# New order of the instructions in phase one of a fused RWKV + mixture-of-experts kernel, and an earlier release of one PSUM tile

## Chip, cores, metric

One core of a Trainium2 chip. The metric is the device time of the whole kernel in microseconds. Before: median 914.38 us of 3 runs (911.5 to 915.5).

## The reference

Two layers, all fp32, on x of 4 x 1024 x 256: an RWKV attention layer with 16 heads of 16 channels, and a mixture of 8 experts with two chosen for each token. Each stands behind a layer norm and inside a residual.

```python
xin = x; x = norm(x)                              # over the 256 channels
xx = shift(x) - x                                # previous token minus this one
r, k, v = (x + xx * maa_r) @ Wr.T, (x + xx * maa_k) @ Wk.T, (x + xx * maa_v) @ Wv.T
g = gelu((x + xx * maa_g) @ Wg.T)
for each chunk of tokens:                        # scan, state is N x N for each head
    y = (r @ k * Wmat) @ v + r @ state * wb
    state = ws * state + (k * wk) @ v
yn = (y - mean(y)) / sqrt(var(y) + eps)          # for each head
x1 = xin + (yn * ln_w + ln_b) * g @ Wo.T
d = norm(x1); probs = softmax(d @ gate.T)        # two experts for each token, 320 places in each for a batch
out = x1 + sum over its experts: probs * (silu(d @ w1) * (d @ w3)) @ w2
```

## The kernel before, in words

Phase one (`phase_a`) works through 4096 tokens in 16 blocks of 256 tokens. For each block it normalizes x (statistics on VectorE `stats1`, rstd on GpSimd `norm1`, scaling on ScalarE `normed1`), transposes it on TensorE (`turn1`, L1187, into the PSUM tile pX), copies it out (`turned1`, L731), mixes it with the shifted x (`shifted`, `mixing` on VectorE, `mixed_g` on GpSimd) and projects r, k, v, g (`project_*`, L1147 and L1172). The attention in a block: `scores` (L1214, two halves a and b, four row tiles of 32 rows each) into pS, `mask` on VectorE (L917, four groups a half), `within` (L1248, four groups a half, column tiles), `across` (L1239, with the state, 32 x 32 tiles), `outer` (L1205, column tiles, the new state's products). y is copied and squared by ScalarE (`keep_y`, `square_y`); `group_sums` (L1261) sums the squares for each head into pX; `group_rstd` (L717, L718) makes 1/sqrt of them as an exponential of a logarithm; then `normed_y` (VectorE), `scaled` (ScalarE), `gated` (GpSimd), `project_o` (L1272), `residual` and `stats2` (VectorE), `norm2` (GpSimd), `normed2` (ScalarE), `turn2` (L1281), `logits` (L1289), `logit_max`, `logit_exp`, `best_two`, `tally`, `count` (L1299, L1300), `slots`, and `scatter`: four indirect DMAs on GpSimd (L564) that send the rows of a block to the expert's places in memory. `weight_high` and `weight_low` split the first expert's weights in two parts, beside all that.

Phase two runs the experts from those places. Its first chunk of 512 rows begins inside phase one's tail (`early_*`).

Each engine runs its own hand-written list of calls, in order: a loop over c, whose calls carry the block that they work on, and a written-out tail. The engines meet only at semaphores. So the order of the lists sets what is late. The loops begin at different values of c, and so how many statistics and normalizations stand ahead of the first block is set there too. The decay tables (`decay_logs` and `bonus` on VectorE, `decay_tables` on ScalarE) are made inside the first turns of the loops.

Two rules of the code matter for the change. pX is one PSUM tile, used in turn by turn1, group_sums and project_o. Before the change turn1 waits for the exponential, though only the logarithm reads pX:

```python
wait(pe, grstd_ready, b - 1)                                     # turn1, L1184
chain.link(nc.scalar.activation(grstd[:], pX[:], ACT.Ln, ...))   # group_rstd, L717
nc.scalar.activation(grstd[:], grstd[:], ACT.Exp, scale=-0.5)    # L718, then grstd_ready
```

And `within(b, 0, 0)` waits for the first mask, `scores_b` for the fourth:

```python
pe.wait_ge(attm_ready[g], TPS * b + t + 1)                       # within, L1246
pe.wait_ge(attm_ready[HGS - 1], TPS * b + 1)                     # scores_b, L1227
```

Of the kernel before, what the change touches and what calls it, by code (L numbers as in the profile page):

```python
# [24 lines left out]
ACT = mybir.ActivationFunctionType  # L25
# [6 lines left out]
N = C // H  # L32
# [228 lines left out]
def phase_a(nc, sb, ps, ctx, sem, ident, x, maa, decay_row, decay_ch, u_row, weights, lnw, lnb, gateT, disp, out,  # L261
# [120 lines left out]
    ysq_ready, ssum_done, yn_ready = sem("ysq_ready"), sem("ssum_done"), sem("yn_ready")  # L382
    y_ready, grstd_ready = sem("y_ready"), sem("grstd_ready")
    z_ready, zg_ready, wo_done = sem("z_ready"), sem("zg_ready"), sem("wo_done")
# [4 lines left out]
    count_done, slot_ready, sent = sem("count_done"), sem("slot_ready"), [sem(f"sent{k}") for k in range(2)]  # L389
    dve_chain, pool_chain, act_chain = sem("dve_chain"), sem("pool_chain"), sem("act_chain")  # L390
    taken_ready = sem("taken_ready")
# [78 lines left out]
    def on_gpsimd(pool):  # L470
# [108 lines left out]

        for c in range(-3, TAIL):  # L580
            scatter(c - 4)
            norm2(c - 2)
            norm1(c + 3)
            if c == -3:
                tables()
            gated(c - 1)
            decayed_r(c + 1)
            mixed_g(c + 1)
            if c == -1:
                empty_rows()  # L590
            weight_low(c - 6)
            chain.reset()

        scatter(11)
        chain.reset()
        norm2(13)
        gated(14)
        weight_low(10)
        scatter(12)
        chain.reset()  # L600
        norm2(14)
        gated(15)
        scatter(13)
        chain.reset()
        norm2(15)
        weight_low(11)
        scatter(14)
        chain.reset()
        early_index()
        scatter(15)  # L610
        chain.reset()
        weight_low(9)

    def on_scalar(act):
        chain = Chain(act, act_chain)
        for dst, src in ((lam_row, decay_row), (lam_ch, decay_ch)):
# [93 lines left out]

        def group_rstd(b):
# [80 lines left out]
        normed2(13)  # L792
        turned2(13)
        keep_y(15)
        square_y(15)
        early_hi(0)
        early_hi(1)
        group_rstd(15)
        logit_exp(13)
        normed2(14)  # L800
        scaled(15)
        early_gate(0)
        turned2(14)
        early_hidden_hi(0)
        early_gate(1)
        weight_high(11)
        early_hidden_hi(1)
        logit_exp(14)
        early_gate(2)
        normed2(15)  # L810
        turned2(15)
        early_hidden_hi(2)
        logit_exp(15)
        early_gate(3)
        early_gate(4)
        early_hidden_hi(3)
        early_hidden_hi(4)
        early_gate(5)
        early_gate(6)
        early_hidden_hi(5)  # L820
        early_hidden_hi(6)

    def on_vector(dve):
# [221 lines left out]

        for c in range(-4, TAIL):
            best_two(c - 3)
            mask(c, 0, 0)
            mask(c, 0, 1)
            mask(c, 0, 2)  # L1050
            mask(c, 0, 3)
            masked_kv(c)
            if c == -1:
                decay_logs()
                center_v()
                head_parity()
            shifted(c + 1)
            mixing(c + 1, 0)
            normed_y(c - 1)
            state_a(c)  # L1060
            tally(c - 3)
            mixing(c + 1, 1)
# [12 lines left out]
            slots(c - 3)  # L1075
            logit_max(c - 2)
            residual(c - 1)
            stats2(c - 1)
            state_b(c)
            chain.reset()  # L1080

        best_two(12)
        mask(15, 0, 0)
        mask(15, 0, 1)
        mask(15, 0, 2)
        mask(15, 0, 3)
        normed_y(14)
        tally(12)
        masked_kv(15)
        state_a(15)  # L1090
        mask(15, 1, 0)
# [4 lines left out]
        chain.reset()  # L1096
        residual(14)
        early_lo(0)
        early_lo(1)
        stats2(14)  # L1100
        logit_max(13)
        normed_y(15)
        best_two(13)
        tally(13)
        slots(13)
        chain.reset()
        early_hidden(0)
        residual(15)
        early_hidden_lo(0)
        early_hidden(1)  # L1110
        logit_max(14)
        stats2(15)
        best_two(14)
        tally(14)
        early_hidden(2)
        early_weight()
        slots(14)
        chain.reset()
        early_hidden_lo(1)
        logit_max(15)  # L1120
        state_b(15)
        best_two(15)
        tally(15)
        early_hidden(3)
        slots(15)
        chain.reset()
        early_hidden_lo(2)
        early_hidden(4)
        early_hidden_lo(3)
        early_hidden_lo(4)  # L1130
        early_hidden(5)
        early_hidden(6)
        early_hidden_lo(5)
        early_hidden_lo(6)
# [3 lines left out]
    def on_tensor(pe):  # L1138
# [192 lines left out]
        for c in range(-1, TAIL):  # L1331
            within(c - 1, 1, 2)
            count(c - 4)
            within(c - 1, 1, 3)
            turn2(c - 3)
            turn_k(c)
            project_o(c - 2)
            logits(c - 3)
            project_v(c)
            group_sums(c - 1)  # L1340
            scores_a(c)
            project_g(c)
# [12 lines left out]
            within(c, 1, 1)  # L1355

        within(14, 1, 2)
        count(11)
        within(14, 1, 3)
        turn2(12)  # L1360
        turn_k(15)
        project_o(13)
        logits(12)
        project_v(15)
        group_sums(14)
        scores_a(15)
        project_g(15)
        outer(15)
        across(15, 0)
        within(15, 0, 0)  # L1370
        scores_b(15)
# [9 lines left out]
        turn2(13)  # L1381
        project_o(14)
        early_turn(0)
        early_turn(1)
        logits(13)
# [12 lines left out]
        early_up(4)  # L1398
        count(15)
        early_up(5)  # L1400
        early_up(6)
# [535 lines left out]
```

## Time and profile before

| | |
|---|---|
| median of 3 runs | 914.38 us (911.5 to 915.5) |
| the profiled execution | 918.7 us, span 917.0 us |
| TensorE matmul busy | 848.2 us (93%) |
| TensorE weight load busy | 706.8 us (77%) |
| VectorE | 460.4 us (50%) |
| ScalarE | 490.7 us (54%) |
| GpSimd | 462.2 us (50%) |
| mean granted TensorE clock | 0.989 |

The span is the time between the first and the last instruction of the profiled execution. Busy time is the time in which an engine works; TensorE's ends are modelled. A row's start is in us from the span's start. In the timelines neighbouring instructions of one form are merged, and a bracket gives the idle time of the engine before the row, and what ended it. A step here is the time between the same instruction of two neighbouring blocks.

### The profile page before, as it was taken

What the parts mean: (1) busy time and instruction counts of PE and PEld (TensorE: products, weight loads), DVE (VectorE), ACT (ScalarE), POOL (GpSimd) and SP (SyncE); (2) the same over time, 40 slices, a digit from 0 to 9 for tenths busy, and PEclk for the clock granted to TensorE, in tenths of its full rate; (3) what the DMA queues carried; (4) which work ended last, traced back from release to release, by engine and by line L of the source; (5) the groups of instructions that cost most, each with busy time, mean ns of one, the idle gap of its engine ahead of it and who ended that gap; (6) DMA issues with size and microseconds to landing.
All of it is one profiled execution on the core that took longest, in us unless ns stands there. A gap on an engine that the chain in (4) does not pass through costs nothing. (4 is left out here: it accounts for less than half of the span.)

```text
span 917.0 us, 18900 instructions
## 1 busy us (share of the span) xinstructions
PE 848.2 (93%) x6791; PEld 706.8 (77%) x6792; DVE 460.4 (50%) x1174; ACT 490.7 (54%) x875; POOL 462.2 (50%) x497
## 2 busy tenths in 40 slices
PE   2899999999999999897999999999799999999995
PEld 1667777777677777787889789879689879889885
DVE  5767777777777766333442342442242443352330
ACT  2578777777788768253443453443353344353331
POOL 4534666677765756456237345237237136447024
PEclk9999999999999999899999999999999999999998
DMA  4572121112211122447025327025225214414013
GB/s 150 223 277 65 49 88 49 49 60 67 81 37 37 37 67 77 158 120 174 1 81 87 112 64 133 3 81 88 72 81 88 71 41 109 90 41 48 13 18 40
DMA packets 50464, 73.94 MB, mean 81 GB/s; under 512 B 5056, under 2 KB 42176, under 8 KB 50368
## 3 DMA queue, kind: packets, MB, share of 16 engines
q1 hardware_dynamic: 35488, 53.46, 17.6%
q0 software_dynamic: 14592, 19.18, 12.3%
q8 instruction: 62, 1.02, 0.4%
q14 instruction: 34, 0.28, 0.1%
q10 hardware_dynamic: 288, 0.01, 0.0%
HBM read 38.41 MB, written 34.22 MB: 79 GB/s over the span
## 5 line engine op out<-in xcount | busy, mean ns | idle before, releaser
L1547 POOL TENSOR_TENSOR wlo<-wraw,whi 128x448 fp32r<-128x448 f32 x84 | 102.6, 1225 | 209.9 <-ACT whi L1604 209.9
L1824 PE MATMUL p<-xh,whi 128*128 128x512 f32 (+1 forms) x504 | 190.9, 379 | 12.8 <-DVE xl L1723 4.9
L1826 PE MATMUL p<-xh,wlo 128*128 128x512 f32 (+1 forms) x504 | 190.4, 378 | 0.0
L1825 PE MATMUL p<-xl,whi 128*128 128x512 f32 (+1 forms) x504 | 189.6, 376 | 0.0
L1741 DVE TENSOR_TENSOR hid<-gated,p 128x512 f32<-128x512 f32 (+1 forms) x126 | 81.1, 643 | 211.6 <-ACT gated L1618 211.6
L1555 POOL DMA_INDIRECT out<-ysb,index x80 | 125.4, 1568 | 91.2 <-ACT ysb L1640 57.3
L1618 ACT ACTIVATE gated<-p 128x512 f32<-128x512 f32 (+1 forms) x126 | 71.0, 563 | 186.3 <-PE p L1826 186.3
L1844 PE MATMUL py<-whi,hh 128*128 128x256 f32 x469 | 135.2, 288 | 6.6 <-DVE hl L1043 3.5
L1846 PE MATMUL py<-whi,hl 128*128 128x256 f32 x469 | 132.6, 283 | 0.0
L1845 PE MATMUL py<-wlo,hh 128*128 128x256 f32 x469 | 132.5, 283 | 0.0
L1824 PEld LDWEIGHTS p<-xh,whi 128*128 128x128 f32 x504 | 95.1, 189 | 33.3 <-issue 11.3
L1825 PEld LDWEIGHTS p<-xl,whi 128*128 128x128 f32 x504 | 95.3, 189 | 18.9
L1826 PEld LDWEIGHTS p<-xh,wlo 128*128 128x128 f32 x504 | 94.9, 188 | 18.9
L1640 ACT ACTIVATE ysb<-py,weight 128x256 f32<-128x256 f32 x67 | 31.8, 475 | 121.7 <-PE py L1846 105.9
L917 DVE TENSOR_TENSOR attm<-pS,dmask 128x512 f32<-128x512 f32 x128 | 79.7, 683 | 32.0 <-remote 22.4
L1844 PEld LDWEIGHTS py<-whi,hh 128*128 128x128 f32 x469 | 89.1, 190 | 7.7 <-DVE hl L1043 3.9
L1749 DVE TENSOR_TENSOR hl<-hid,hh 128x512 fp32r<-128x512 f32 (+1 forms) x126 | 88.9, 706 | 3.7 <-ACT hh L1627 3.1
L1845 PEld LDWEIGHTS py<-wlo,hh 128*128 128x128 f32 x469 | 89.1, 190 | 0.4
L1846 PEld LDWEIGHTS py<-whi,hl 128*128 128x128 f32 x469 | 89.1, 190 | 0.0
L564 POOL DMA_INDIRECT disp<-row,slot_i x64 | 65.0, 1015 | 42.4 <-DVE slot_i L1025 26.3
L1723 DVE TENSOR_TENSOR xl<-pt,xh 128x512 fp32r<-128x512 f32 x33 | 22.7, 691 | 110.9 <-ACT xh L1610 103.2
L1627 ACT CAST hh<-hid 128x512 fp32r<-128x512 f32 (+1 forms) x126 | 72.8, 577 | 1.1 <-DVE hid L1741 1.1
(195 smaller groups left out, 1417.7 us busy)
## 6 DMA issues: line engine op xcount, KB each, us to landing
wraw<-in_w SPq DMA_DIRECT2D x24, 896.0 KB
disp<-wraw SPq DMA_DIRECT2D x16, 662.5 KB, 8.9
xtok<-disp SPq DMA_DIRECT2D x16, 530.0 KB, 5.1
x_ring<-in_x SPq DMA_DIRECT2D x16, 256.0 KB, 3.0
out<-x SPq DMA_DIRECT2D x16, 256.0 KB
xtok<-disp SPq DMA_DIRECT2D x8, 265.0 KB, 6.0
out<-ysb,index POOLq DMA_INDIRECT x80
disp<-row,slot_i POOLq DMA_INDIRECT x64
```

The costliest lines, as they stand in the source:

```text
L917: nc.vector.tensor_tensor(attm[g][:], pS[:, :, g // 2, g % 2, :], group_mask(g), ALU.mult).then_inc(attm_ready[g], 1)
L1547: nc.gpsimd.tensor_tensor(wlo[e.const % 2][m][:, cut], wraw[k][:, cut], whi[e.const % 2][m][:, cut].bitcast(F32), ALU.subtract).then_inc(w ...
L1555: nc.gpsimd.indirect_dma_start(out, bass.IndirectOffsetOnAxis(ap=index[e.const % 2][:, t:t + 1], axis=0), ysb[j % NY][:], None, compute_op ...
L1627: nc.scalar.copy(hh[(u * NCH + q) % 2][:, f, 0:w], hid[k][:, 0:w]).then_inc(hh_ready, 1)
L1741: nc.vector.tensor_tensor(hid[k][:, 0:w], gated[k][:, 0:w], p3[k][:, 0:w], ALU.mult).then_inc(hid_ready, 1)
L1749: nc.vector.tensor_tensor(hl[s][:, f, 0:w], hid[k][:, 0:w], hh[s][:, f, 0:w].bitcast(F32), ALU.subtract).then_inc(hl_ready, 1)
L1824: nc.tensor.matmul(dst[:, 0:w], hi[m][:, wcut], xh[xcut], start=(kt == 0), stop=False)
L1825: nc.tensor.matmul(dst[:, 0:w], hi[m][:, wcut], xl[xcut], start=False, stop=False)
L1826: ins = nc.tensor.matmul(dst[:, 0:w], lo[m][:, wcut], xh[xcut], start=False, stop=(kt == KT - 1))
L1844: nc.tensor.matmul(py[j % 2][:, 0:C], a, hi[:, cut], start=(f == 0), stop=False)
L1845: nc.tensor.matmul(py[j % 2][:, 0:C], a, lo[:, cut], start=False, stop=False)
L1846: ins = nc.tensor.matmul(py[j % 2][:, 0:C], b, hi[:, cut], start=False, stop=(f == FT - 1))
```

## The change

On TensorE the order of a step becomes: logits, turn_k, project_v, group_sums, scores_a, across, outer, within 0,0, turn1, project_g, scores_b, within 0,1 and 0,2, across, within 0,3, project_r, project_k, within 1,0 to 1,2, count, within 1,3, turn2, project_o. `group_rstd` is split, and turn1 waits for the logarithm's new semaphore. The lists of the other engines are reordered, their loops begin one turn later (GpSimd -2 instead of -3, VectorE -3 instead of -4), and with it the first blocks have one statistics less ahead. The work done is the same.

```diff
+        def group_log(b):
             if 0 <= b < STEPS:
                 act.wait_ge(ssum_done, b + 1)
...
                 wait(act, yn_ready, b)
-                chain.link(nc.scalar.activation(grstd[:], pX[:], ACT.Ln, scale=1.0 / N, bias=gn_eps[:, 0:1]))
+                nc.scalar.activation(grstd[:], pX[:], ACT.Ln, scale=1.0 / N, bias=gn_eps[:, 0:1]).then_inc(grlog_ready, 1)
+
+        def group_rstd(b):
+            if 0 <= b < STEPS:
+                act.wait_ge(grlog_ready, b + 1)
                 nc.scalar.activation(grstd[:], grstd[:], ACT.Exp, scale=-0.5).then_inc(grstd_ready, 1)
...
                 pe.wait_ge(xn_ready, b + 1)
-                wait(pe, grstd_ready, b - 1)
+                wait(pe, grlog_ready, b - 1)
```

TensorE's loop:

```diff
         for c in range(-1, TAIL):
-            within(c - 1, 1, 2)
-            count(c - 4)
-            within(c - 1, 1, 3)
-            turn2(c - 3)
+            logits(c - 3)
             turn_k(c)
-            project_o(c - 2)
-            logits(c - 3)
             project_v(c)
             group_sums(c - 1)
             scores_a(c)
+            across(c, 0)
+            outer(c)
+            within(c, 0, 0)
+            turn1(c + 1)
             project_g(c)
-            turn1(c + 1)
-            outer(c)
-            across(c, 0)
-            within(c, 0, 0)
             scores_b(c)
             within(c, 0, 1)
             within(c, 0, 2)
-            project_r(c + 1)
             across(c, 1)
             within(c, 0, 3)
+            project_r(c + 1)
             project_k(c + 1)
             within(c, 1, 0)
             within(c, 1, 1)
+            within(c, 1, 2)
+            count(c - 3)
+            within(c, 1, 3)
+            turn2(c - 2)
+            project_o(c - 1)
```

ScalarE's loop:

```diff
         for c in range(-2, TAIL):
+            logit_exp(c - 3)
+            weight_high(c - 4)
+            value(c)
+            group_log(c - 1)
+            group_rstd(c - 1)
             turned1(c + 1)
-            normed1(c + 2)
             column(c + 1)
             gate(c)
             scaled(c - 1)
             normed2(c - 2)
-            receptance(c + 1)
             if c == -1:
                 decay_tables()
             pairs(c + 1)
+            receptance(c + 1)
             key(c + 1)
+            normed1(c + 2)
+            turned2(c - 2)
+            square_y(c)
             keep_y(c)
-            square_y(c)
-            turned2(c - 2)
-            logit_exp(c - 2)
-            value(c + 1)
-            group_rstd(c)
-            weight_high(c - 4)
```

VectorE's and GpSimd's loops:

```diff
-        for c in range(-4, TAIL):
...
+        for c in range(-3, TAIL):
             mask(c, 1, 0)
             mask(c, 1, 1)
             mask(c, 1, 2)
             mask(c, 1, 3)
+            state_b(c)
             mixing(c + 1, 2)
-            stats1(c + 4)
+            slots(c - 3)
+            stats1(c + 3)
+            residual(c - 1)
+            logit_max(c - 2)
+            stats2(c - 1)
             if c == -1:
                 bonus(0)
             decayed_k(c + 1)
             if c == -1:
                 bonus(1)
                 slot_tables()
...
+            best_two(c - 2)
+            tally(c - 2)
+            mask(c + 1, 0, 0)
+            mask(c + 1, 0, 1)
+            mask(c + 1, 0, 2)
+            mask(c + 1, 0, 3)
+            masked_kv(c + 1)
+            state_a(c + 1)
+            if c == -2:
+                decay_logs()
+                center_v()
+                head_parity()
+            shifted(c + 2)
+            mixing(c + 2, 0)
+            normed_y(c)
+            mixing(c + 2, 1)
...
-        for c in range(-3, TAIL):
+        for c in range(-2, TAIL):
             scatter(c - 4)
             norm2(c - 2)
-            norm1(c + 3)
-            if c == -3:
+            norm1(c + 2)
+            if c == -2:
                 tables()
             gated(c - 1)
             decayed_r(c + 1)
+            weight_low(c - 6)
             mixed_g(c + 1)
             if c == -1:
                 empty_rows()
-            weight_low(c - 6)
```

The tails are reordered in the same way; on TensorE one more early product stands before turn2 of blocks 14 and 15.

```diff
         early_up(0)
         early_up(1)
         count(13)
+        early_up(2)
         turn2(14)
         project_o(15)
         logits(14)
-        early_up(2)
         early_up(3)
+        early_up(4)
         count(14)
         turn2(15)
         logits(15)
-        early_up(4)
+        early_up(5)
         count(15)
-        early_up(5)
         early_up(6)
```

## Rows read from the trace of the kernel before

**Rows 1.** Busy time by stretches: from:to, length, busy time of each engine, granted clock.

```profile
46.50:328.60 282.10, 268.41 (x3173) 203.09 (x3172) 212.79 (x676) 217.99 (x353) 179.71 (x235) 1.00 0.22 73
328.60:344.80 16.20, 14.09 (x205) 10.33 (x204) 10.34 (x33) 11.68 (x17) 8.74 (x13) 1.00 0.28 93
344.80:380.00 35.20, 29.94 (x130) 23.58 (x128) 22.44 (x90) 23.31 (x38) 21.25 (x29) 0.90 0.19 67
```

**Rows 2.** Waits, 0 to 400 us: who waited for whom, us, times, longest.

```profile
PE pX L1187 <- ACT grstd L718: 11.8, 14, 0.8
```

**Rows 3.** Timeline of TensorE, one step: start, length, what, [idle before].

```profile
205.39 1.03 PE L1261 MATMUL pX<-ysq,blockdiag 128*128 128x256 f32 x4
206.35 1.15 PE L1214 MATMUL pS<-r_pair,kT 32*128 32x256 f32 x16
207.43 1.99 PE L1147 MATMUL pB<-mixed,w_in_sb 128*128 128x256 f32 x8
210.26 0.63 PE L1187 MATMUL pX<-ident,xn 128*128 128x128 f32 x4 [0.84 <-ACT grstd L718]
210.82 0.46 PE L1205 MATMUL pA<-v_pad,k_dec 128*32 128x32 f32 x32
211.21 0.64 PE L1239 MATMUL pY<-r_dec,state 32*32 32x128 f32 x16
211.78 0.42 PE L1248 MATMUL pY<-attm,v_pad 128*32 128x128 f32 x8
212.53 1.15 PE L1214 MATMUL pS<-r_pair,kT 32*128 32x256 f32 x16 [0.33 <-DVE attm L917]
...
226.00 1.03 PE L1261 MATMUL pX<-ysq,blockdiag 128*128 128x256 f32 x4
```

**Rows 4.** Timeline of ScalarE in the same step.

```profile
205.59 0.59 ACT L699 COPY v_pad<-pA 128x512 f32<-128x512 f32 x1 [1.19 <-PE pA L1172]
...
207.49 0.69 ACT L717 ACTIVATE grstd<-pX,gn_eps 128x512 f32<-128x512 f32 x1
...
209.49 0.63 ACT L718 ACTIVATE grstd<-grstd 128x512 f32<-128x512 f32 x1
...
217.28 1.26 ACT L653 ACTIVATE r_pair<-pA,parity 128x512 f32<-128x512 f32 x2
```

**Rows 5.** Timeline of VectorE in the same step, the four masks of the first half.

```profile
210.00 2.48 DVE L917 TENSOR_TENSOR attm<-pS,dmask 128x512 f32<-128x512 f32 x4 [2.56 <-remote]
```

**Rows 6.** Timeline of TensorE and VectorE in block 1, before any scatter.

```profile
46.52 1.15 PE L1214 MATMUL pS<-r_pair,kT 32*128 32x256 f32 x16
...
47.74 2.48 DVE L917 TENSOR_TENSOR attm<-pS,dmask 128x512 f32<-128x512 f32 x4 [2.68 <-PE pS L1214]
```

**Rows 7.** Timeline of GpSimd: mixed g, then first and last of four indirect DMAs.

```profile
200.62 1.09 POOL L543 TENSOR_TENSOR mixed<-mixed,xT 128x512 f32<-128x512 f32 x1
...
204.13 1.11 POOL L564 DMA_INDIRECT disp<-row,slot_i  x1 [1.19 <-DVE slot_i L1025]
...
208.10 0.97 POOL L564 DMA_INDIRECT disp<-row,slot_i  x1 [0.30 <-issue]
```

**Rows 8.** Timeline of the start, 12 to 33 us.

```profile
12.06 0.75 DVE L875 BATCH_NORM_STATS2 st<-x_ring 128x6 f32<-128x256 f32 x2 [2.21 <-DMA x_ring<-in_x]
...
13.27 2.29 DVE L839 TENSOR_TENSOR dmask<-lam_row,lag 128x2048 f32<-128x2048 f32 x1
...
19.00 3.57 PE L1147 MATMUL pA<-mixed,w_in_sb 128*128 128x256 f32 x8 [9.69 <-DVE mixed L898]
...
22.61 0.59 ACT L644 COPY rT<-pA 128x512 f32<-128x512 f32 x1 [9.83 <-PE pA L1147]
...
25.68 0.19 ACT L628 ACTIVATE sdecay<-lam_ch 128x2 f32<-128x2 f32 x1
...
26.92 0.58 ACT L661 COPY kT<-pB 128x512 f32<-128x512 f32 x1
...
30.27 2.31 DVE L866 SCALAR_TENSOR_TENSOR dmask<-ident,u_sb,dmask 128x128 f32<-128x128 f32 x8
```

More of the change, by code:

```diff
@@ L382, in phase_a @@
     ysq_ready, ssum_done, yn_ready = sem("ysq_ready"), sem("ssum_done"), sem("yn_ready")
-    y_ready, grstd_ready = sem("y_ready"), sem("grstd_ready")
+    y_ready, grlog_ready, grstd_ready = sem("y_ready"), sem("grlog_ready"), sem("grstd_ready")
     z_ready, zg_ready, wo_done = sem("z_ready"), sem("zg_ready"), sem("wo_done")
@@ L389, in phase_a @@
     count_done, slot_ready, sent = sem("count_done"), sem("slot_ready"), [sem(f"sent{k}") for k in range(2)]
-    dve_chain, pool_chain, act_chain = sem("dve_chain"), sem("pool_chain"), sem("act_chain")
+    dve_chain, pool_chain = sem("dve_chain"), sem("pool_chain")
     taken_ready = sem("taken_ready")
@@ L596, in on_gpsimd @@
         norm2(13)
+        weight_low(10)
         gated(14)
-        weight_low(10)
         scatter(12)
@@ L601, in on_gpsimd @@
         norm2(14)
+        weight_low(9)
         gated(15)
@@ L605, in on_gpsimd @@
         norm2(15)
-        weight_low(11)
         scatter(14)
         chain.reset()
-        early_index()
         scatter(15)
         chain.reset()
-        weight_low(9)
+        early_index()
+        weight_low(11)
     def on_scalar(act):
-        chain = Chain(act, act_chain)
         for dst, src in ((lam_row, decay_row), (lam_ch, decay_ch)):
@@ L709, in normed1 @@
                 ins.then_inc(xn_ready, 1)
-        def group_rstd(b):
+        def group_log(b):
             if 0 <= b < STEPS:
@@ L780, in on_scalar @@
             pairs(c + 1)
+            receptance(c + 1)
             key(c + 1)
+            normed1(c + 2)
+            turned2(c - 2)
+            square_y(c)
             keep_y(c)
-            square_y(c)
-            turned2(c - 2)
-            logit_exp(c - 2)
-            value(c + 1)
-            group_rstd(c)
-            weight_high(c - 4)
+        logit_exp(12)
+        value(15)
+        group_log(14)
+        group_rstd(14)
+        normed2(13)
         scaled(14)
         gate(15)
-        normed2(13)
         turned2(13)
@@ L797, in on_scalar @@
         early_hi(1)
+        group_log(15)
+        logit_exp(13)
         group_rstd(15)
-        logit_exp(13)
+        early_gate(0)
         normed2(14)
         scaled(15)
-        early_gate(0)
+        weight_high(11)
+        early_gate(1)
         turned2(14)
+        early_gate(2)
         early_hidden_hi(0)
-        early_gate(1)
-        weight_high(11)
+        logit_exp(14)
         early_hidden_hi(1)
-        logit_exp(14)
-        early_gate(2)
+        early_gate(3)
         normed2(15)
@@ L813, in on_scalar @@
         logit_exp(15)
-        early_gate(3)
         early_gate(4)
         early_hidden_hi(3)
+        early_gate(5)
         early_hidden_hi(4)
-        early_gate(5)
+        early_hidden_hi(5)
         early_gate(6)
-        early_hidden_hi(5)
         early_hidden_hi(6)
@@ L1044, in early_hidden_lo @@
                                     ALU.subtract).then_inc(hl_ready, 1)
-        for c in range(-4, TAIL):
[L1047 to L1062, printed above, removed]
+        for c in range(-3, TAIL):
             mask(c, 1, 0)
@@ L1074, in on_vector @@
                 slot_tables()
[L1075 to L1079, printed above, removed]
-            chain.reset()
[L1082 to L1090, printed above, removed]
+            best_two(c - 2)
[14 more added lines that the diff above has]
+            mixing(c + 2, 1)
+            chain.reset()
         mask(15, 1, 0)
@@ L1097, in on_vector @@
         residual(14)
+        stats2(14)
         early_lo(0)
         early_lo(1)
-        stats2(14)
         logit_max(13)
-        normed_y(15)
         best_two(13)
         tally(13)
+        early_hidden(0)
+        normed_y(15)
         slots(13)
         chain.reset()
-        early_hidden(0)
+        early_hidden(1)
         residual(15)
+        stats2(15)
+        logit_max(14)
         early_hidden_lo(0)
-        early_hidden(1)
-        logit_max(14)
-        stats2(15)
+        early_hidden(2)
         best_two(14)
         tally(14)
-        early_hidden(2)
-        early_weight()
+        early_hidden_lo(1)
         slots(14)
         chain.reset()
-        early_hidden_lo(1)
+        early_weight()
+        early_hidden(3)
         logit_max(15)
-        state_b(15)
+        early_hidden_lo(2)
         best_two(15)
         tally(15)
-        early_hidden(3)
+        early_hidden(4)
         slots(15)
         chain.reset()
-        early_hidden_lo(2)
-        early_hidden(4)
         early_hidden_lo(3)
+        early_hidden(5)
+        state_b(15)
         early_hidden_lo(4)
-        early_hidden(5)
+        early_hidden_lo(5)
         early_hidden(6)
-        early_hidden_lo(5)
         early_hidden_lo(6)
@@ L1355, in on_tensor @@
             within(c, 1, 1)
[L1357 to L1360, printed above, removed]
+            within(c, 1, 2)
[3 more added lines that the diff above has]
+            project_o(c - 1)
+        logits(12)
         turn_k(15)
-        project_o(13)
-        logits(12)
         project_v(15)
@@ L1366, in on_tensor @@
         scores_a(15)
+        across(15, 0)
+        outer(15)
+        within(15, 0, 0)
         project_g(15)
-        outer(15)
-        across(15, 0)
-        within(15, 0, 0)
         scores_b(15)
@@ L1382, in on_tensor @@
         project_o(14)
+        logits(13)
         early_turn(0)
         early_turn(1)
-        logits(13)
         group_sums(15)
```

## Prediction

> **What bounds the kernel now.** I read the page first: the change touches phase one alone, about the first 380 of 917 us, so only there can time be won. Then the busy time by stretches [rows 1]: from the scores of block 1 to those of block 15 (46.5 to 328.6 us) TensorE is busy 268.41 of 282.10 us at a granted clock of 1.00, and the next engine 217.99. So phase one is TensorE's instruction stream plus 13.7 us in which it stands still. The waits name most of that [rows 2]: 11.8 us in 14 waits of the transposes of x (L1187) for ScalarE's exponential (L718). The other 1.9 us are mostly short waits of the second scores (L1214) for VectorE's masks.
>
> One step of TensorE [rows 3] repeats after 20.6 us. The reader is to see the two bracketed waits in it, 0.84 before L1187 and 0.33 before the second L1214. ScalarE shows where the first is from [rows 4]: copy of v at 205.59, table load, logarithm until 208.18, table load, exponential until 210.12; TensorE goes on at 210.26. The transposes overwrite the sums in PSUM, which only the logarithm reads: the exponential works in SBUF.
>
> The second wait has an odd source. The first scores are over by their row at 207.50, yet the masks begin at 210.00 [rows 5], with VectorE idle for 2.56 us. In block 1 they began at 47.74, 0.07 us after the scores' 47.67, in the same order of instructions [rows 6]. What is new in between is GpSimd: four indirect DMAs, from 204.13 to 209.07 [rows 7]; the masks begin 0.93 us after the last. So the completion of the scores is seen late while GpSimd issues scatters. The rows don't say whether the full-array product that follows the scores has a part in it.
>
> **The change, part by part.** (1) *Release by the logarithm.* The transposes now wait for 208.18 instead of 210.12, 1.94 us earlier. In the new order they also come sooner: after the sums at 205.39 stand the scores, across, outer and one group of within: by the starts in [rows 3] 0.96+1.08+0.57+0.39+0.42 = 3.4 us, so 208.8. The logarithm is 0.6 us ahead of that: the 0.84 goes in all 14 steps, 11.8 us.
>
> (2) *New order on TensorE.* No matmul is added or left out. In a step the first scores no longer stand before the g product but before across. Within 0,0 now stands 1.08+0.57+0.39 = 2.04 us after the scores' start and needs the first mask: scores 1.15, mask about 0.7 (a quarter of 2.48 plus its pipeline [rows 5]), some 0.1 for signals: 1.95. It just fits, if the completion is seen at once. The second scores come after transposes 0.56 and the g product 1.99, at 2.04+0.42+0.56+1.99 = 5.0, and the fourth mask is over at 1.15+2.48+0.1 = 3.7: the 0.33 goes too. Together 13.7 us if nothing takes its place.
>
> The cost of a switch between kinds of products I take as nothing: scores to across is not in any row. A step has two fewer changes of shape, which at the 0.1 us by which neighbouring starts differ would be 0.2 a step at best; on the other side stands the late completion, priced below as a rival. The Trainium skill's page "TensorEngine Tiling (Array Packing)", section "Key Properties", says that a change of tiling mode drains TensorE. By it the sum would be a little better, by those two switches (some 3 us over 15 steps, my estimate from the rows); no row here separates the drain, so I leave it out.
>
> (3) *ScalarE.* The four table loads stay four. The move of normed1 behind the key fills waits for products, and the whi cast goes into the wait before v. Pairs (1.26 us [rows 4]) now stand before rT, so rT comes 1.2 later, and with it r_dec and, behind it on GpSimd, weight_low (1.1) and then mixed_g. Mixed g was ready at 200.62+1.09 = 201.71 for a product at 207.43 [rows 3, 7]: 5.7 us of slack against 2.3 lost and 0.5 by its earlier neighbours. Covered, as are the rows that GpSimd's later scatters read. normed1 no longer makes norm1 wait on GpSimd.
>
> (4) *VectorE.* Slots now stand right after the last mixing and wait for count, with the loop's statistics and the residual behind them. Laid on TensorE's new step this leaves the engine idle some 2.9 us before slots; the first to feel it is decayed_k, which I find 1.2 us ahead of the scores. It has 212.79 us of work in 282.10, so room.
>
> (5) *The start.* This is the part that the title doesn't tell [rows 8]. Today VectorE does the third statistics (2.21 us of waiting for x, then 1.0) before the decay logarithms, and ScalarE does the decay tables (four exponentials, from 23.2 to 25.87) only after rT, which waited 9.83 us for the first r product. In the new loops only two statistics stand ahead, and the tables stand before pairs and rT, so in ScalarE's idle time. Decay logarithms begin 3.2 earlier, the r product at 15.8 instead of 19.00; the tables are over near 15.2. Then pairs, rT and kT follow the products directly, with kT over near 21.7 instead of 27.50: 5.8 us. The bonus on the mask ends at 32.58 today, and follows kT through its transposes and decayed_k. GpSimd's mixed_g will run beside it, so I take 5.0; bounds 3.2 (the statistics alone) and 6.2 (all waits gone).
>
> (6) *The tail.* From 328.6 to 344.8 TensorE idles 2.1 us, from 344.8 to 380 another 5.3, with a clock of 0.90 there [rows 1]. The new order puts early products into such waits, but the chains behind the last block (normalization, scatter, hidden) are as long as before. I take 2.0; bounds -2 and +6.
>
> Sum against the profiled execution's own 918.7 us: 13.7+5.0+2.0 = 20.7, so 898.0. That execution stands 4.3 us above the median of the runs, 914.4; on the median's scale it is 893.7, and I say 894.
>
> **Rivals.** *The completion stays late (slower).* If the scatters alone hold back the signal, it falls on the path: within 0,0 waits for the first mask, and transposes, g product and everything else behind it. GpSimd's four DMAs would stand at much the same place relative to the scores, or up to 1 us later. The signal would come 2.4 to 3.3 us late, within 0,0 starts 2.3 to 3.3 us later (3.0 taken), against 1.2 saved, in 12 steps, the blocks from 4 on, whose scores stand beside a scatter: 12 x 3.0 = 36 us on top of 894, so 930. It decides from about 1.7 us of lateness; below that the start's gain still covers it. For it: in [rows 6] the scores were followed by the same product and nothing was late, so the scatter is necessary. Against: whether it is sufficient is not shown, and the full-array products that end beside the first scatters release ScalarE at once (v at 205.59). Chance 0.15.
>
> *It stays late in part.* Should it be freed after the third DMA, 1.2 to 1.5 us late, half of that wait remains: 12 x 1.4 = 17 us, 911. Chance 0.1.
>
> *Only the steady steps gain.* Should the start be held by something that the rows hide (the bonus's mask beside GpSimd's work, or the zero rows that SyncE writes), 5 us are missing, and with a tail that gives nothing, 901. Chance 0.2.
>
> *The release by the logarithm does nothing* because the g product itself is the late one: then 0.84 a step stays, 12 us, 906. For it: its completion may be hidden behind the same scatters. Against: the wait is 0.84 also in block 1, before any scatter. It shares the 0.1 of the partial case.
>
> **How the numbers follow.** Forecast case 0.55, 889 to 898 by its bounds. Only the steady steps 0.2, partial or late g product 0.1, late completion 0.15. The range 887 to 911 leaves out the late completion and a little at the lower end. A measurement here tells 0.5%, 4.6 us, from no change. Faster by more than that, under 909.8: the forecast, the steady case and half of the partial cases, 0.80. Within it: 0.06. Slower: the late completion, 0.14.
>
> **What would show it.** Right: in a steady step no wait before L1187, none before the second L1214, TensorE's step near 19.4 us instead of 20.6; VectorE's first mask of a block within 0.1 us of the scores' end although the scatters run; the first kT over at about 22 instead of 27.50 us. Wrong: a wait of 1 us or more before the first L1248 of a block, released by VectorE's mask, with the mask itself waiting for the scores beside GpSimd's DMAs; or a first r product still at 19 us; or decayed_k late for the first scores.

## The result, and the profile after

The changed kernel took 892.98 us (median of four runs, 892.45 to 894.43), the kernel before 914.89 us beside it: a ratio of 0.977, 95% interval [0.9743, 0.9798]. The prediction said 894. That is the result on record. It isn't the whole of it. An occasion is here a set of runs made together on one chip, with the kernel before timed beside them. Timed twice more, unaltered, on two other occasions and two different chips, the same kernel took 926.01 us (ratio to the kernel before 1.0113 [1.009, 1.0135]) and 926.16 us (1.0098 [1.0073, 1.0124]). On each occasion the runs of the changed kernel agree within 0.3%, and the median of the kernel before stayed between 914.9 and 918.9 us on all five occasions. All times are medians of fast runs; of the variant with the old start a fourth run, at 2941 us, was slow and is left out. Most of what follows is about these 33 us.

First the profile of the execution on record, busy time by stretches (from:to, length, then PE, PEld, DVE, ACT, POOL, granted clock, share of the DMA engines, GB/s). The first row goes from the scores of block 1 to those of block 15, the second to the end of that block's work on TensorE:

```profile
42.10:303.00 260.90, 260.61 (x3177) 203.24 (x3176) 213.77 (x687) 220.17 (x354) 175.09 (x241) 1.00 0.22 77
303.00:318.20 15.20, 14.17 (x207) 10.69 (x207) 10.74 (x29) 11.61 (x17) 11.02 (x14) 1.00 0.36 117
318.20:354.00 35.80, 29.21 (x137) 24.25 (x136) 20.34 (x85) 22.52 (x37) 19.74 (x28) 0.89 0.19 61
```

Against [rows 1] the reader is to see that TensorE no longer stands still: 0.3 us in 14 steps where it was 13.7, and from block 4 on a step of 18.8 us (one of 19.2) where it was 20.1 to 20.9. Its busy time has also gone down, by 7.8 us with the same instructions. One step of TensorE, beside [rows 3] (start, length, what; no bracket means no wait):

```profile
208.00 1.03 PE L1261 MATMUL pX<-ysq,blockdiag 128*128 128x256 f32 x4
208.96 1.15 PE L1214 MATMUL pS<-r_pair,kT 32*128 32x256 f32 x16
210.04 0.64 PE L1239 MATMUL pY<-r_dec,state 32*32 32x128 f32 x16
210.61 0.46 PE L1205 MATMUL pA<-v_pad,k_dec 128*32 128x32 f32 x32
210.98 0.43 PE L1248 MATMUL pY<-attm,v_pad 128*32 128x128 f32 x8
211.34 0.66 PE L1187 MATMUL pX<-ident,xn 128*128 128x128 f32 x4
```

VectorE's masks in that step, beside [rows 5]:

```profile
210.23 2.48 DVE L926 TENSOR_TENSOR attm<-pS,dmask 128x512 f32<-128x512 f32 x4 [0.64 <-PE pS L1214]
```

The scores are over at 210.11 and the mask begins at 210.23, 0.12 us later, although GpSimd is in the middle of its four transfers by index:

```profile
207.65 1.10 POOL L564 DMA_INDIRECT disp<-row,slot_i  x1 [0.87 <-POOL row L559]
209.06 0.97 POOL L564 DMA_INDIRECT disp<-row,slot_i  x1 [0.31 <-issue]
210.34 0.97 POOL L564 DMA_INDIRECT disp<-row,slot_i  x1 [0.30 <-issue]
211.61 0.97 POOL L564 DMA_INDIRECT disp<-row,slot_i  x1 [0.31 <-issue]
```

So it is in each block from 4 to 15 but one. In block 6 the first mask began 0.50 us after the scores, and there stands the one wait of these 14 steps, 0.29 us before within 0,0.

The start, beside [rows 8]: TensorE's r product, ScalarE's tables, now ahead of the pairs, and the first scores with the one wait behind them:

```profile
15.44 3.40 PE L1147 MATMUL pA<-mixed,w_in_sb 128*128 128x256 f32 x8 [6.14 <-DVE mixed L907]
...
23.56 1.15 PE L1214 MATMUL pS<-r_pair,kT 32*128 32x256 f32 x16
...
27.39 0.42 PE L1248 MATMUL pY<-attm,v_pad 128*32 128x128 f32 x8 [1.73 <-DVE attm L926]
```

```profile
12.03 1.91 ACT L623 ACTIVATE dmask<-dmask 128x2048 f32<-128x2048 f32 x1 [1.88 <-DVE dmask L848]
...
20.61 0.59 ACT L660 COPY kT<-pB 128x512 f32<-128x512 f32 x1
```

And the tail, where phase two begins with a wait for the last piece of GpSimd's low weights, which the new order puts behind the last scatter:

```profile
351.82 0.55 PE L1839 MATMUL py<-whi,hh 128*128 128x256 f32 x1 [5.62 <-POOL wlo L549]
```

The gain of 26.1 us in the span (917.0 to 890.9) divides by the starts of the first scores and of py. Up to block 1 (46.52 to 42.12): 4.4. Fourteen steps (282.1 to 260.8): 21.3, of which 13.4 are waits and 7.8 busy time. From the scores of block 15 to py (51.35 to 48.86): 2.5. Phase two lost 2.1 (536.98 to 539.11).

### The profile page after: what moved, and what is told of

It is laid out like the page before. It is cut to its first block and busy times, and to the rows that moved or that the text cites. A ratio compares the mean times of both kernels' runs of the same rounds, so it can differ in the third digit from the quotient of the medians.

```text
span 890.9 us, 18900 instructions
## 1 busy us (share of the span) xinstructions
PE 840.5 (94%) x6791; PEld 708.4 (80%) x6792; DVE 457.9 (51%) x1174; ACT 492.1 (55%) x875; POOL 455.9 (51%) x497
## 5 line engine op out<-in xcount | busy, mean ns | idle before, releaser
L564 POOL DMA_INDIRECT disp<-row,slot_i x64 | 64.5, 1007 | 32.7 <-issue 14.5
```

## Experiments

The open question after this profile was why VectorE, which before the change began its first mask 1.2 to 2.7 us after the scores' end in the blocks from 4 on, now began it 0.12 us after. "The completion is seen late" means this time between the end of the scores' row and the start of the mask. The first theory was adjacency: a completion is seen late where a full-array product follows the 32-row scores, and at once where another small product does.

**The release by the logarithm alone**, on the kernel before:

```diff
-                wait(pe, grstd_ready, b - 1)
+                wait(pe, grlog_ready, b - 1)
```

> The kernel before with the release by the logarithm alone. If the late completion of the scores is real and TensorE itself is not held (theory A): the transposes start right behind the g product, about 1.0 us earlier a step, but the second scores still wait for the masks, whose start is fixed by the end of the scatters, so in blocks 4 to 15 the wait before the second scores grows from 0.3 to about 1.3 us and only blocks 1 to 3 gain: -3 us in the profile. If the lateness is a product of profiling alone (rival), the profile shows that, but the median of the timed runs falls by about 14 us. If the g product's own late completion holds TensorE (second rival), the wait before the transposes stays near 0.7 us.

Measured: 914.72 us, ratio 0.9945 [0.9928, 0.9962], so 4.2 us. The waits of TensorE from 100 to 327 us show why it isn't 11.8 (who waited for whom, us, times, longest):

```profile
PE pS L1214 <- DVE attm L917: 12.0, 11, 1.3
```

The wait before the transposes is gone and another stands in its place, 1.1 us a step: the second scores wait for masks that began late because the first scores' completion was seen late. Steps from block 7 on stay at 20.6 to 20.9 us; the steps gain 3.6 us in all between blocks 1 and 5, before and just after the transfers set in. So the lateness that looked free in the kernel before was already next in line.

**Across directly behind the scores**, on the kernel before, and **both together**:

```diff
             scores_a(c)
+            across(c, 0)
             project_g(c)
             turn1(c + 1)
             outer(c)
-            across(c, 0)
```

> The kernel before with one call moved: across of the first half stands between the first scores and the g product. Theory A (a full-array product directly behind the row-tiled scores, beside a scatter, is what makes their completion late): VectorE's first mask starts within 0.15 us of the scores' end in blocks 4 to 15 as well, the wait before the second scores goes, the transposes still wait for the exponential; about -0.9 us a step, -12 us. Rival (the scatters alone make it late): the first mask still starts 1 to 2.5 us late, the second scores still start when the fourth mask is done, and the time is within 2 us of before.

> Both edits together on the kernel before. Theory A: no wait is left before the transposes or the second scores; -1.3 us a step or a little more by one tiling switch less, about -18 us. If the scatters alone make the completion late: as the release alone, -3 us.

Measured: 918.54 us, ratio 0.999 [0.9972, 1.0009], and 915.24 us, 0.9961 [0.9943, 0.9979]. In both the first mask of a block from 4 on began 1.4 to 2.8 us after the scores' end, as before. The adjacency theory falls: a small product behind the scores doesn't bring their completion in time.

**The scatter later**, on the kernel before:

```diff
-            scatter(c - 4)
             norm2(c - 2)
+            scatter(c - 4)
             norm1(c + 3)
```

> The kernel before with the four scatters of a step moved behind norm2 on GpSimd, so that they begin about when the first scores end. If a running scatter is needed for the lateness: the first mask starts within 0.15 us of the scores' end in nearly all blocks though the g product still stands behind them, and the wait before the second scores goes or shrinks; norm1 comes later by 5 us, which its slack covers: -3 to -5 us. If the adjacency alone is enough from block 4 on: first mask as late as before, time the same.

Measured: 955.62 us, ratio 1.0401 [1.0374, 1.0428]. A gain of 3 to 5 us was expected; it lost 37. The first mask now began 0.12 us after the scores in blocks 4 to 14, with the transfers starting 0.9 us after their end, but the steps were 22.5 us, and 24.1 where the granted clock was 0.93 over the step. The transfers hit what came next. TensorE in one step (bracket: idle before, and its cause):

```profile
203.21 0.46 PE L1205 MATMUL pA<-v_pad,k_dec 128*32 128x32 f32 x32
203.59 1.08 PE L1239 MATMUL pY<-r_dec,state 32*32 32x128 f32 x14
204.99 0.37 PE L1239 MATMUL pY<-r_dec,state 32*32 32x128 f32 x2 [0.32 <-issue]
205.29 0.30 PE L1248 MATMUL pY<-attm,v_pad 128*32 128x128 f32 x1
205.75 0.27 PE L1248 MATMUL pY<-attm,v_pad 128*32 128x128 f32 x1 [0.16 <-issue]
206.45 0.47 PE L1248 MATMUL pY<-attm,v_pad 128*32 128x128 f32 x6 [0.43 <-issue]
```

the first and the last of the four transfers beside it:

```profile
200.75 1.10 POOL L564 DMA_INDIRECT disp<-row,slot_i  x1 [0.87 <-POOL row L559]
204.73 0.97 POOL L564 DMA_INDIRECT disp<-row,slot_i  x1 [0.30 <-issue]
```

and VectorE, which needs the outer products that ended at 203.67:

```profile
206.60 0.29 DVE L923 TENSOR_TENSOR kvm<-pA,parity 128x128 f32<-128x128 f32 x1 [4.11 <-remote]
```

Sixteen across products that take 0.64 us elsewhere now take 1.8, and a completion is seen 2.9 us late. "Issue" says that TensorE waited for nothing that the profile shows, and this is read as TensorE having no instruction to run. The outer products themselves took their 0.46 us in the midst of the transfers here, behind the four full-array transposes; the gaps came in what followed them. So standing beside a transfer is not enough by itself to stretch a run of small products: how much has run just before seems to count too, which no run tests.

**Four variants of the changed kernel**, on another occasion (the kernel before 916.26 us there). *The exponential releases the transposes again:*

```diff
-                wait(pe, grlog_ready, b - 1)
+                wait(pe, grstd_ready, b - 1)
```

> The changed kernel, but the transposes wait for the exponential again. The exponential ends 1.4 us behind the transposes' present start, so a wait of 1.4 us before them in each of 14 steps: +20 us on the changed kernel, 913. If some of the waits behind it have slack that takes it up (it has none on TensorE), less.

*The g product directly behind the scores, where it was:*

```diff
             scores_a(c)
+            project_g(c)
             across(c, 0)
             outer(c)
             within(c, 0, 0)
             turn1(c + 1)
-            project_g(c)
```

> The changed kernel, but the g product stands directly behind the first scores again (then across, outer, within 0,0, transposes). Theory A: the first mask starts about 2.4 us late in the blocks from 4 on, and the second scores wait for the fourth mask, 2.0 to 2.5 us a step; blocks 1 to 3 lose nothing but two tiling switches: +25 to +30 us, 918 to 923. If the place of the scatters relative to the scores had cured it (rival): first mask at once, +0 to +4 us.

*The old start:* stats1(2) ahead of decay_logs on VectorE, receptance(0) ahead of decay_tables on ScalarE.

```diff
             if c == -2:
+                stats1(2)
                 decay_logs()
...
             if c == -1:
+                receptance(0)
                 decay_tables()
```

> The changed kernel with the old start: the third statistics again ahead of the decay logarithms, rT again ahead of the decay tables. By my working the start is worth 4.4 to 5 us: first scores at about 30 us instead of 23.6, scores of block 1 at about 46.5 to 48; 897 to 898. The steps behind are as in the changed kernel, 18.8 us.

*The gaps of start and tail filled:*

```diff
             if c == -1:
                 bonus(0)
+                bonus(1)
             decayed_k(c + 1)
...
+        weight_low(11)
         scatter(15)
         chain.reset()
         early_index()
-        weight_low(11)
```

(and slot_tables moved one block later, ahead of slots).

> The changed kernel with its remaining avoidable waits attacked: the bonus on the mask wholly ahead of decayed_k of block 0 and the slot tables later (the first mask of block 0 at about 24.9 instead of 26.65 us, the wait of 1.73 us before within 0,0 gone, and with it perhaps the slow clock of the g product there, 1.4 us more); weight_low(11) ahead of the last scatter (the wait before the first product of phase two 5.6 down to about 3.5 us). Together -3 to -5 us: 888 to 890. If the clock and the tail's chain behind it take it back: -1.

Measured, in that order: 931.61 us (1.0172 [1.0129, 1.0215]), 910.23 (0.9934 [0.9913, 0.9955]), 930.95 (1.0158 [1.0106, 1.021]), 923.54 (1.008 [1.0049, 1.011]). The g product behind the scores came out 8 us under its range: from block 4 on its first masks began 0.8 to 1.8 us after the scores, and the second scores waited for them only once, 0.3 us. The other three miss upwards, by 19 to 34 us, and, odder, a variant with a better start and tail lost 30 us. In block 4, the first beside a scatter, its VectorE, ScalarE, GpSimd and SyncE stand within 0.02 us of those of the kernel on record, instruction by instruction, for the 4 us before VectorE waits for the scores. Then their completion comes 0.8 us later than it did there, and the outer products, 0.46 us on record, take 2.2. The edits of that variant lie in the start and in the tail, far from here. That made two theories: the edits bring it in some way, or it was the occasion.

**The changed kernel unaltered, and with the smallest edit of the last variant:**

```diff
+        weight_low(11)
         scatter(15)
         chain.reset()
         early_index()
-        weight_low(11)
```

> The changed kernel again, unaltered, on the chip of the two runs below. In the traces of the starts and bonus variants the 64 instructions of the outer products (L1205) took 2.0 to 3.1 us beside the send's transfers where the changed kernel took 0.46 us, although both engines stood within 0.02 us of one another up to that point. Theory P (property of the program): unaltered it runs as before, 892 to 895 us, outer products 0.46 us in all blocks, steps 18.8 us. Theory R (property of the run: chip, or where the program and its buffers lie): here too the outer products may stall, 2 to 3 us from block 4 on, steps 21 to 23 us, 915 to 935 us.

> The changed kernel with weight_low(11) ahead of scatter(15) on GpSimd, the smallest edit of the variant of 923.5 us. Theory P: phase one as in the changed kernel up to block 15; in the tail wlo ends some 4 us earlier, of which the 5.6 us wait of py on it gives back 2 to 4 us: 889 to 892. If theory P holds in the form that any edit to GpSimd's order brings the stall: 915 to 925. Theory R: this run goes as the unaltered kernel beside it does, less 2 to 4 us, whichever way that is.

Measured: 926.01 us and 924.56 us (1.0091 [1.0065, 1.0117]). It was the occasion, and not the edits. The same kernel that ran at 892.98 now ran 33 us longer. Its profile in one step, TensorE first:

```profile
222.52 0.39 PE L1214 MATMUL pS<-r_pair,kT 32*128 32x256 f32 x4
222.84 0.64 PE L1239 MATMUL pY<-r_dec,state 32*32 32x128 f32 x16
223.41 0.32 PE L1205 MATMUL pA<-v_pad,k_dec 128*32 128x32 f32 x12
223.99 0.24 PE L1205 MATMUL pA<-v_pad,k_dec 128*32 128x32 f32 x3 [0.26 <-issue]
224.73 0.26 PE L1205 MATMUL pA<-v_pad,k_dec 128*32 128x32 f32 x4 [0.49 <-issue]
225.44 0.19 PE L1205 MATMUL pA<-v_pad,k_dec 128*32 128x32 f32 x1 [0.46 <-issue]
226.16 0.33 PE L1205 MATMUL pA<-v_pad,k_dec 128*32 128x32 f32 x11 [0.53 <-issue]
```

```profile
220.47 1.10 POOL L564 DMA_INDIRECT disp<-row,slot_i  x1 [0.87 <-POOL row L559]
221.89 0.97 POOL L564 DMA_INDIRECT disp<-row,slot_i  x1 [0.31 <-issue]
223.17 0.97 POOL L564 DMA_INDIRECT disp<-row,slot_i  x1 [0.30 <-issue]
224.44 0.97 POOL L564 DMA_INDIRECT disp<-row,slot_i  x1 [0.30 <-issue]
```

```profile
224.77 2.48 DVE L926 TENSOR_TENSOR attm<-pS,dmask 128x512 f32<-128x512 f32 x4 [2.38 <-remote]
```

The transfers stand to the scores as in the profile on record (first one 2.4 us before their end, last one 1.5 after). But the 32 outer products, which with their 32 weight loads took 0.46 us there, take 3.1 us here: a few at a time, some 0.7 us apart, and freely again 0.75 us after the last transfer is issued (225.41). The first mask begins 1.86 us after the scores' end, where it was 0.12. The stretches of this execution:

```profile
41.00:331.80 290.80, 274.37 (x3177) 211.16 (x3176) 214.83 (x687) 221.05 (x354) 170.33 (x241) 0.98 0.21 71
331.80:384.80 53.00, 43.70 (x334) 34.23 (x333) 31.54 (x114) 34.35 (x53) 30.23 (x41) 0.91 0.21 73
384.80:923.60 538.80, 513.88 (x3051) 453.88 (x3051) 184.21 (x294) 220.09 (x436) 230.15 (x173) 0.98 0.33 76
```

So the 14 steps take 290.8 us where the record has 260.9: 29.9 more. The outer products of blocks 4 to 14 take 2.0 to 3.1 us instead of 0.46. From the start of the first of them to the start of the product behind them it is 29.2 us in these 11 blocks, and 4.5 on record: 24.7 more. Three of the steps are 1.7 us longer again, 23.1 instead of 21.4, and those have the lower clock:

```profile
177.30:198.70 21.40, 19.68 (x229) 15.10 (x228) 15.93 (x52) 16.27 (x27) 13.50 (x19) 1.00 0.15 51
198.70:221.80 23.10, 21.39 (x233) 16.24 (x232) 16.12 (x52) 16.17 (x27) 13.61 (x19) 0.93 0.16 49
```

That is 5.1 us; 24.7 + 5.1 = 29.8 against 29.9. The rest of the 32.7 us of span is in block 15 and the tail (4.2 more), less 1.1 in the start. Phase two is the same (538.8 against 539.1).

**The transfers moved away from the small products**, in the variant with filled gaps:

```diff
-            scatter(c - 4)
             norm2(c - 2)
             norm1(c + 2)
...
             gated(c - 1)
+            scatter(c - 4)
```

> The variant of 923.5 us (bonus and slot tables moved, weight_low(11) earlier) with scatter(c-4) moved behind gated(c-1) in the loop on GpSimd, so that the four transfers by index are issued beside the r and k products (128-row matmuls, one per 0.1 us) instead of beside the 112 instructions of across, outer and within (7 to 20 ns each). Theory X (the transfers hold back TensorE's supply of instructions, which only a stretch of small tiles feels): outer products 0.46 us again in blocks 4 to 14, first scores seen within 0.05 us, steps 18.8 to 19.5 us (r_dec up to 3 us later, in time for the next block), 888 to 900. Rival Y (the stall is no matter of the transfers, but of what TensorE finds ahead of its small tiles): outer products still 2 us or more, 915 to 930.

Measured: 982.77 us, ratio 1.0736 [1.0704, 1.0769], a clear miss in time. But the mechanism came out as theory X had it. The outer products, one step:

```profile
202.70 0.61 PE L1214 MATMUL pS<-r_pair,kT 32*128 32x256 f32 x8
203.24 0.64 PE L1239 MATMUL pY<-r_dec,state 32*32 32x128 f32 x16
203.81 0.46 PE L1205 MATMUL pA<-v_pad,k_dec 128*32 128x32 f32 x32
```

They took 0.46 us in all blocks from 4 to 14, and the first mask began 0.12 us after the scores, on an occasion on which the same products, beside the transfers, took 3 us. The time went to a wait that the edit itself brought in:

```profile
220.28 1.11 PE L1281 MATMUL pS<-ident,row 128*128 128x128 f32 x4 [5.43 <-ACT row L635]
```

ScalarE's normed2 writes the row buffer that the scatter of two blocks earlier still sends, and stood waiting for 9.3 us for it. (The trace names no releaser; the wait is read from the code, where normed2 waits for the sends of that buffer.) Two row buffers are too few for a later scatter. The last of these transfers fell into TensorE's own wait, so this run doesn't show how the products beside which they were meant to stand would have borne them.

**The changed kernel a third time**, on another chip than the runs just told:

> The changed kernel a third time, unaltered. The first time it took 892.98 us with outer products of 0.46 us and signals seen at once, the second time, on another occasion, 926.01 us with outer products of 2.0 to 3.1 us beside the transfers and signals up to 1.8 us late; within each occasion all runs agree within 0.3%. Theory R (two states of the chip or of where the run's memory lies, fixed for all runs of an occasion): one of the two figures again, 892 to 895 or 924 to 928, nothing between, and the length of the outer products tells which. Rival (a third cause that varies more finely, such as the time at which the loads come): a time between, with outer products stalled in some blocks only.

Measured: 926.16 us, with steps that agree with those of the second time within 0.1 us, and outer products of 2.0 to 3.1 us. Two times are seen and nothing between. Counting the variants, whose outer products took 2.0 to 3.1 us too where they keep the changed order and the place of the transfers, the hold-up was there on chips 1, 14 and 3, and it was absent only in the result on record.

## Why the prediction was right, and how far

**Bound and steady steps.** Both waits went as said, 0.84 and 0.33 us a step. The term was too small: 13.7 forecast, 21.3 measured. The working priced the switches between kinds of products at nothing, with 0.2 us a step as the most. The rows after show about 0.4: from start to start the eight products of r, k and v take 1.84, 1.82 and 1.73 us where they took 1.92, 1.92 and 1.81, the transposes of x 0.49 where they took 0.56, within some 0.07 less. With the end of the g product (1.99, now 1.82) that makes up the 7.8 us of busy time. The 0.08 of v is no change of tiling: both before and after it stands between full-array products, behind the logits before and behind transposes now. The rest is 0.32 a step, 4.5 us in 14. The Trainium skill's page "TensorEngine Tiling (Array Packing)", section "Key Properties", says that changing the tiling mode drains TensorE. The trace agrees in sign, and the prediction's estimate of 3 us by it was low. No run here moved a switch by itself, so the size is read, not shown.

**"It just fits, if the completion is seen at once."** On the record it was, and the first mask came 0.12 us after the scores. That condition was the step that carried everything, and it doesn't hold on every occasion. On two of three the rival that was given 0.15, *the completion stays late*, came true. It was priced at 930 and measured at 926, but that nearness is in part luck. The completion was 0.7 to 1.8 us late and not 2.4 to 3.3, and its mechanism was only half right: within 0,0 hardly waited for the mask (0.2 us, once); TensorE was held earlier, in the outer products, for want of instructions. Of the 33 us about 5 are the lower clock, which the rival left out. The prediction also left out that the outer products are the stretch with the most instructions in the least time, 64 in 0.46 us, and that the change moves them from 1.7 us after the last transfer's end [rows 3, 7] into the midst of the transfers. The kernel before gave a hint that the prediction did not read, in its block 15: there the outer products stood 1.1 us behind the last transfer's start, and had a gap:

```profile
331.65 0.39 PE L1205 MATMUL pA<-v_pad,k_dec 128*32 128x32 f32 x22
332.36 0.35 PE L1205 MATMUL pA<-v_pad,k_dec 128*32 128x32 f32 x10 [0.32 <-issue]
```

**Release by the logarithm.** 11.8 us was right only in the company of the new order. Alone it gave 4.2, because the late masks stood behind it. Taken out of the changed kernel it cost 5.6 (931.61 against 926.01, on different chips, both with the hold-up), 4.6 of it in the three steps from block 1 to 4, each 1.5 us longer; from block 4 on the wait was hidden in the stall of the outer products.

**Start.** 5.0 forecast, 4.4 in the record's profile. The old start put back cost 4.9 us (930.95 against 926.01, on different chips), and block 1 began at 47.1 instead of 41.0 to 41.8. The term holds; on the record a granted clock of 0.5 for 3.41 us, from 28.56 on, behind the first wait, took part of it.

**Tail.** 2.0 forecast, 2.5 measured up to py, less 2.1 in phase two, which the change doesn't touch and in which the granted clock was 0.98 instead of 0.99: its half-speed stretches fell elsewhere. Putting weight_low(11) ahead of the last scatter gave 1.4 us, 926.01 to 924.56, not more than the intervals allow for nothing.

**The sum.** 20.7 forecast, 26.1 in the spans. The two profiled executions flatter the change: that of before was 4.3 above its median, as the prediction took into account, that of after 0.3 below. On the scale of the profiled executions the forecast was 898.0 and the measurement 892.66: too slow by 5.3, with a steady term 7.6 too small against 2.1 lost in phase two. The 4.3 taken off for the scale hid most of that, since the profiled execution after had no such excess. So that 894 stands 1 us from 892.98 is luck; what was right is the two waits and the start, and the condition as it held on record. The range held the record. The two later times, at 926, lie outside it.

**What stays open.** What differs between the occasions is not shown: the chip, or where the run's instructions and buffers lie in memory, or something else. The second time and the third were on different chips, and which chip the first was on isn't known. In the trace of the kernel before, completions are late from block 4 on. Its profiled execution, 918.7 us, lies above all four runs timed on the record's occasion (911.5 to 915.5) and among those of the later ones (912.5 to 920.7). Both suggest that it was recorded under the worse condition, and that a little of the 26.1 us between the two profiles belongs to the occasion; neither shows it, since there is no trace of that kernel under the better one. For the same reason no experiment ran under the condition of the result on record: its gain is read from its own trace, and its parts were tested under the other condition alone. That TensorE is starved of instructions is inferred from "issue" and from the spacing; the 16 KB packets that load instructions take 0.9 to 1.8 us on record and 0.9 to 1.6 the second time, at like places of the stream, so the starving isn't in them as far as the profile records.

Of the versions tried, the one with the g product between scores and across is the best under the worse condition: 910.23 against 916.26 of the kernel before and 926 of the changed one. There the g product keeps the small products behind most of the transfers (the last starts 0.2 to 1.3 us before the outer products, which take 0.8 to 1.9 us in blocks 4 to 14). Whether it also comes to 893 under the better condition wasn't seen.

## What to carry to other kernels

Keep runs of tiny TensorE products clear of GpSimd's indirect DMAs: 64 instructions in half a microsecond took 2.0 to 3.1 beside them, where the eight full-array products of g in the kernel before took 1.99 us beside them as in block 1 without. A wait that is removed pays only what the next late thing leaves, so look for completions that come late now and cost nothing yet. And when one order is sensitive to something the profile can't name, time the same file on a second occasion before believing either figure.

## What the runs showed of the hardware that was not expected

- One file, at 893 us on one occasion and at 926 us on two others, with runs of each agreeing within 0.3%, while another order of the same work moved by 0.3% between the same occasions (914.89, 917.0 and 917.61).
- While GpSimd issues an indirect DMA, TensorE's completions may be seen 0.7 to 2.9 us late, and its stream of short instructions may come in bursts some 0.7 us apart. The last burst begins 0.75 us after the last transfer is issued (226.16 after 225.41). The completions come at other times: in the second profile of the changed kernel 0.8 to 1.9 us after the scores' end, while the third or the fourth transfer is issued (the fourth ends 2.5 after it), and in the kernel before up to 1.0 us behind the end of the last.
- The hold-ups went with a second cost by the clock: in the steady steps on record TensorE ran without a wait and the granted clock was 1.00 throughout; in steps with 2.6 us of hold-up it was 1.00 and 0.93 by turns from block 8 on. In such a step the granted clock was 0.50, the lower level of 1.2 GHz, for about 3.4 us (from 204.1 to 207.4), and those steps are 1.7 us longer. That the hold-up brings the lower clock is read from their coming together; in the variant with the g product first, hold-ups of up to 1.5 us left it at 1.00 in the steady steps.
